# Layer 3's edge stage: column numbers read from a PSUM bank, turned attributes of both steps in one bank

## The reference

```python
x = concatenate([node[src], node[dst], edge_attr])          # 64 + 64 + 32 per edge
h = relu(x @ W1.T + b1)
messages = h @ W2.T + b2
agg = segment_sum(messages, dst)
r, z = sigmoid(i_r + h_r), sigmoid(i_z + h_z)                # gi = agg @ w_ih.T, gh = node @ w_hh.T
n = tanh(i_n + r * h_n);  out = (1 - z) * n + z * node
```

## Time and profile before

| | us |
|---|---|
| median of three executions | 9233.94 |
| span of the profiled execution | 9369.1 |
| layer 3's edge stage in it, from 7285 to 9183 | 1898 |
| POOL's gathers in that stage, 1020 | 1315.0 busy |

### The profile page before, as it was taken

How to read it: one execution, slowest core, us unless ns; L and a number is a source line. 1 busy time by engine, 2 the same in 40 slices (tenths; PEclk the granted TensorE clock), 3 DMA queues, 4 the chain that set the end, 5 groups by cost and what they waited for, 6 DMA issues and landing times. The chain is left out here.

```text
span 9369.1 us, 138875 instructions
## 1 busy us (share of the span) xinstructions
PE 5537.1 (59%) x49076; PEld 4542.6 (48%) x49077; DVE 5345.0 (57%) x9166; ACT 1663.2 (18%) x3235; POOL 4789.4 (51%) x4394
## 2 busy tenths in 40 slices
PE   2555555555555523233455542899996677777777
PEld 1333333333333322223345441899995566666665
DVE  5555655565556533334344455666665677777773
ACT  0111111111111100002111131000002333333333
POOL 3555555555555454550355551455550577667670
PEclk7666676666666666665666675999996788888885
DMA  3222222221222154441100030111110333333330
GB/s 98 77 82 78 73 75 81 78 78 70 81 78 80 40 92 89 88 88 29 42 20 19 20 109 12 26 26 27 27 27 17 106 100 97 95 93 95 95 92 13
DMA packets 392774, 612.74 MB, mean 65 GB/s; under 512 B 158383, under 2 KB 318995, under 8 KB 377363
## 3 DMA queue, kind: packets, MB, share of 16 engines
q1 hardware_dynamic: 240826, 478.03, 16.7%
q0 software_dynamic: 141056, 124.52, 6.4%
q10 hardware_dynamic: 10454, 4.04, 0.2%
HBM read 531.52 MB, written 216.25 MB: 80 GB/s over the span
## 5 line engine op out<-in xcount | busy, mean ns | idle before, releaser
L321 POOL DMA_INDIRECT pay_d<-row,place x1632 | 1719.7, 1054 | 1524.9 <-DVE place L497 947.9
L415 PE MATMUL win<-onehot,val 128*128 128x128 f32 x4998 | 1045.4, 353 | 672.4 <-issue 455.3
L415 PEld LDWEIGHTS win<-onehot,val 128*128 128x128 f32 x4998 | 872.3, 251 | 926.8 <-issue 644.4
L514 DVE TENSOR_TENSOR onehot<-near_dve,drel 128x896 f32<-128x896 f32 x357 | 389.3, 1091 | 1182.2 <-remote 1057.4
L2113 POOL DMA_INDIRECT m_from_src<-from_src_d,m_row x510 | 684.0, 1341 | 628.5 <-issue 375.4
L1712 PE MATMUL g_win<-g_hot,y_part 128*128 128x128 bf16 x14994 | 880.7, 220 | 145.1 <-DVE g_hot L1761 101.1
L1692 POOL DMA_INDIRECT g_x<-xg_d,g_row x510 | 641.5, 1258 | 625.1 <-PE g_win L1712 411.7
L1712 PEld LDWEIGHTS g_win<-g_hot,y_part 128*128 128x128 bf16 x14994 | 857.3, 99 | 166.8 <-DVE g_hot L1761 102.1
L1091 POOL DMA_INDIRECT sorted_d<-s_row,s_place x510 | 494.1, 969 | 531.0 <-DVE s_place L1207 368.5
L672 POOL DMA_INDIRECT r_x<-in_x,r_row x510 | 485.2, 951 | 500.9 <-DMA r_row<-pay_d 351.2
L2116 POOL DMA_INDIRECT m_from_dst<-from_dst_d,m_row x510 | 631.0, 1237 | 160.0 <-issue 155.7
(11 more groups left out here) (410 smaller groups left out, 11491.4 us busy)
## 6 DMA issues: line engine op xcount, KB each, us to landing
m_hot_t<-drow_d SPq DMA_DIRECT2D x52, 1568.0 KB
scan_d<-in_none SPq DMA_DIRECT2D x51, 1034.2 KB
lo_row<-lo_d SPq DMA_DIRECT2D x51, 1024.0 KB
m_grid<-pay_d SPq DMA_DIRECT2D x52, 882.0 KB
pay_d<-in_fill SPq DMA_DIRECT2D x51, 882.0 KB
grid<-pay_d SPq DMA_DIRECT2D x51, 882.0 KB, 3.8
pay_d<-in_fill SPq DMA_DIRECT2D x51, 720.0 KB
row<-in_pay SPq DMA_DIRECT2D x51, 576.0 KB
```

The lines of the kernel that those rows point to most:

```text
L321: pool.indirect_dma_start(a["pay_d"][:, :], bass.IndirectOffsetOnAxis(ap=place[j][:, c:c + 1], axis=0), row[j][:, c, :], None).then_inc(ro ...
L415: mm(win[:, :], val[u % 2][:, s, :], onehot[u % 2][:, s, :], start=(u == 0 and s == 0), stop=(u == NS - 1 and s == SUB - 1))
```

## The change

The two attribute buffers become the halves of one bank, the bank that this frees takes both sets of column numbers, and DVE's two comparisons read them there. DVE fills them once, ahead of the first block. Since PE may not write a bank while ACT reads it, `turn_in` of every step now waits for both copies of the step before; till now only those of two steps before had to be made.

```diff
-        ea_ps = [ps(f"m_ea_ps{u}", [P, 512]) for u in range(2)]
+        ea_bank = ps("m_ea_ps", [P, 2, 2 * P])
+        ea_ps = [ea_bank[:, u, :] for u in range(2)]
+        near = ps("m_near_dve", [P, 512])
+        numbers, steps = near[:, 0:W], near[:, W:W + WS]
...
                 def turn_in(n, j, u):
-                    pe.wait_ge(copied, n * (2 * NS) + (2 * u + 1 if u else 3))
+                    pe.wait_ge(copied, n * (2 * NS) + (2 * u + 3))
...
                 def bf_hot(n, j, u):
-                    v.tensor_tensor(hot[u][:, :, :], k.iota[:, :].unsqueeze(1).to_broadcast([P, SUB, W]),
+                    v.tensor_tensor(hot[u][:, :, :], numbers.unsqueeze(1).to_broadcast([P, SUB, W]),
...
                 def expand():
-                    v.tensor_tensor(onehot[:, :, :], k.steps[:, :].unsqueeze(1).to_broadcast([P, SC, WS]),
+                    v.tensor_tensor(onehot[:, :, :], steps.unsqueeze(1).to_broadcast([P, SC, WS]),
...
+                v.tensor_copy(numbers, k.iota[:, :])
+                v.tensor_copy(steps, k.steps[:, :])
+                dve.drain()
                 mark(0, 0, 0)
```

## The result

The changed kernel takes 9265.9 us (median of 9 executions, 9253.7 to 9285.2) against 9238.6 us for the kernel before (9 executions beside them): ratio 1.0032, 95% interval 1.0021 to 1.0043. That is 27 us slower: a small difference that is clear of the noise, more than the forecast of 9244 but inside its range of 9206 to 9282.

The account below looks back on a forecast made before the run. No engine alone was taken as the bound: PE, ACT and DVE hand a step round in a ring. Step 0's wait +15, PSUM -1 and delay made good -4 add +10 us to 9233.9: 9244 us, range 9206 to 9282.

Parts of the forecast that it names:

- The relief of POOL: POOL's gathers in the edge stage lose about 210 us of busy time; worth 0, as their reader never waits.
- PE's "issue" rows: Time in which PE waits for no engine, 135.1 us before line 2149; moving by over 20 us would show the forecast wrong.
- PSUM as a source: DVE's comparisons reading column numbers from PSUM: -1 us in sum, bounds -5 and +2; a little dearer, 3%.
- DVE held by POOL: Rival: POOL's gathers held DVE's instructions, so DVE gains; about -10 us, 9239 in all, 5%; the forecast took 0.
- Step 0's wait, +15 us: At each block's head PE's transposes come after ACT's copies: 0.29 us in each of 51 blocks, with nothing hiding it.
- "Nothing hides it": At a block's head DVE is idle, 1.43 us in the block read, so the delay of step 0 passes on in full.
- the sign that the prediction named: If right, DVE's wait before each block's first line 2291 grows by 0.3 us.
- Steps 2 and 3, 0: The new wait there costs PE +30 us, hidden by its 2.29 us before `reduce` and DVE's work in hand; taken as 0.
- three times a block: Sign if right: PE's line 2135 waits for ACT's line 2229 about that often, at steps 0, 2 and 3.
- Sum: Whole change in the edge stage: +15 - 1 - 4 = +10 us, giving 9244 us, +0.1%.

Follow-up runs that it names:

- kind Q: Three of the four chips of the follow-up experiments; the kernel before takes 7637 to 7649 us there.
- kind P: One of the four chips of the follow-up experiments; the kernel before takes 9389 us there, near the first measurement's 9239 us.

## Why the range held, and which steps of the forecast failed

The range held in part by luck: the first measurement fell on a slow chip. On kind Q the same change is worth -113 us, far below a range reaching 28 us down, and the forecast's mechanism has no term for it.

- *The relief of POOL.* Its size was right (1088.7 us against 1105), and on kind P so was its worth: nothing. The argument, that no one waits for the gathers, was read from an execution in which a block takes 37.5 us (1915 over 51), more than the 31.8 us of its 20 gathers and gaps. It isn't a property of the kernel. On kind Q, where the block before the change takes 34.0 us, it is worth 107 us by itself. The prediction had the row for it: 1315 us of gathers and 1020 gaps of 0.30 us make 1621 of 1915 us; and it saw PE's "issue" rows, but asked only whether they would shrink, not what would bound the block without them.
- *PSUM as a source.* Right: 1083 against 1086 ns in the mean, 1825 against 1825. The 65 ns more per instruction that the Trainium skill, "VectorE: DVE Perf Modes", "The TRN2 errata", leads to are in no run.
- *DVE held by POOL.* Right to take 0: the longest comparison fell from 1156 to 1093 ns, the median by 2, and in the kernel before the 262 comparisons of line 2285 that started under a gather have a median of 1084 ns, the 99 others 1083. The lock of the Trainium skill, "SBUF — State Buffer", "Who interferes with whom", shows on POOL's side alone.
- *Step 0's wait, +15 us.* This step failed. PE's price is 0.12 us in the block read, not 0.23. And on kind Q DVE's idle time before its first sum is not a wait for PE but its own two register loads, which hide the price: no run there shows a cost. "Nothing hides it" was the wrong reading. In the slow profiles that time is longer than the loads (the first sum starts over 1.7 us after the window sum in 39 of 50 heads before the change, in 8 of 50 on kind Q), so PE's product can come last there. But the sign that the prediction named, 0.3 us more per block, is absent: leaving out the stage's first sum, the 50 idle times add up to 140.5 us before and 140.7 after. On kind P they make 123.8 us with the numbers alone, 135.1 with step 0's wait and 123.9 with the whole change, so the +10 us of the run by itself is not settled by the profiles either.
- *Steps 2 and 3, 0.* About right: +4 to +7 us with an interval that holds 0. PE's transposes waited for ACT 93 times in 51 blocks, not three times a block: in some 48 blocks at step 0 and some 37 at step 3, but in only 9 at step 2.
- *Sum.* On kind P the parts make 1.0005, +0.0012 and +0.0004, so 1.0021, and the whole measured 1.0012: they agree within their intervals, and both with the forecast of +10 us. The first measurement's +27 us (by the ratio's interval 19 to 40) is larger than either, and its cause stays open: none of the parts was run beside it. One candidate that the prediction had no term for is the 14 us of DVE's first sum. It waits 19.1 to 20.9 us in all five slow profiles of a changed kernel, 5.4 us in the one slow profile of the kernel before and 3.5 to 4.2 us in the eight of kind Q. What releases it the profile doesn't name, and as kind P has no profile of the kernel before, it isn't shown that the change causes it. PE's "issue" rows in the stage moved by more than the 20 us that the prediction named as a sign against it: those before line 2149's weight loads from 135.1 to 54.0 us, all of PE's own matmul rows together from 286 to 310. But this is between two profiled executions whose other stages differ as much.

The numbers in PSUM with two banks for the attributes (7531.5 us on kind Q, no change on kind P) are the safer version where both kinds count: the whole change is 10 us behind the kernel before on kind P and was 27 us behind at the first measurement, where the numbers alone weren't run. Against each other the two aren't told apart on either kind: 1.0005 and 1.0012 on kind P, 0.9858 and 0.9853 on two chips of kind Q.

## What to carry to other kernels

Before a relief of an engine is priced at nothing because no one waits for it, add its busy time and its gaps and hold the sum against the stage. Where it comes near (here 1621 of 1915 us, and 1696 of 1736 on another chip) it may be the next bound, and slowness of another engine may be all that hides it. An idle time put down to a semaphore can be the engine's own register loads; it is then cover for whatever comes late from elsewhere. The longest single wait of a row is worth a look by itself: it can be one event of the stage's start and not a cost of every block. A change of this size is measured on more than one chip before it is kept or dropped.

## What the runs showed of the hardware

- Chips differ by more than the change. The same program took 9239 us at the first measurement, 9389 us on one chip and 7637 to 7649 us on three others; where it is slow PE pauses between instructions that wait for nothing (455.3 us before the products of line 415 alone, at most 4 us on kind Q), and its granted clock is lower (0.73 to 0.74 against 0.80 to 0.81). What makes PE pause isn't shown.
- A gather whose indices lie in SBUF waits for the end of a VectorE instruction with two SBUF operands and not for one that reads a PSUM operand: 0.94 us clear, 1341 and 1237 ns in the mean before, 1122 and 1013 after. The 71 gathers that started inside line 2307's comparison of 1600 took 1.65 to 2.41 us before; the 84 that did so after took 0.94 to 0.95. It waits as well for line 2327's comparison in place, bfloat16 with one tensor and a column of SBUF: on kind Q the 51 gathers that started in it have a median of 2.46 us. The VectorE instruction isn't lengthened.
- Loading one register from SBUF takes VectorE's queue 0.30 us, and two loads with their checks fill 1.36 us of idle time at the head of a block, more than the 0.12 us that was to be paid there.
